# First expert layer hands twelve scatters instead of eight to the weight chain behind it; the chain's third-round loads wait for scatters, and rows are measured by halves

## The reference, cut to what matters

```
x = x + tanh(g_xattn[0]) * _L0_xattn_ref(_layernorm(x), ctx, ...)
x = x + tanh(g_ffn[0])   * _L0_ffn_ref(_layernorm(x), ...)      # 16 experts, 6 per row, and a shared expert
x = x + tanh(g_xattn[1]) * _L1_xattn_ref(_layernorm(x), ctx, ...) # 16 heads, latent keys and values
...
```

## Time and profile before

| | us |
|---|---|
| median of 3 runs | 963.36 |
| lowest, highest | 956.77, 964.65 |
| the profiled execution's own time | 961.0 |
| its span | 959.2 |

### The profile page before, as it was taken

The page is one execution under the profiler, slowest core; times in us unless marked ns, Lnnn a source line. Parts: engine busy times, 40 slices in busy tenths (PEclk is TensorE's granted clock), DMA queues, the critical chain, the costliest instruction groups (busy, mean ns, idle before and its releaser), DMA issues. The chain is left out here.

```text
span 959.2 us, 15375 instructions
## 1 busy us (share of the span) xinstructions
PE 895.2 (93%) x5046; PEld 711.2 (74%) x5046; DVE 585.4 (61%) x1069; ACT 356.2 (37%) x635; POOL 448.9 (47%) x347
## 2 busy tenths in 40 slices
PE   7999999998899999999978997999889989899997
PEld 4899997885666666666757984868647868788886
DVE  6788888557544443443366988667687746582322
ACT  3454553321033333443244534444315443322321
POOL 5787784002267887887531222271038013363233
PEclk9999999997799999999888999999999998999999
DMA  8412110009647546554622001010000027753321
GB/s 321 136 52 90 46 46 1 1 21 390 260 78 167 83 75 155 83 84 59 168 88 88 1 2 39 1 40 2 1 21 34 1 74 246 242 190 51 48 42 12
DMA packets 39893, 84.86 MB, mean 88 GB/s; under 512 B 9885, under 2 KB 27677, under 8 KB 37310
## 3 DMA queue, kind: packets, MB, share of 16 engines
q1 hardware_dynamic: 23358, 64.56, 20.1%
q0 software_dynamic: 16176, 19.31, 12.3%
q10 hardware_dynamic: 288, 0.07, 0.0%
HBM read 71.23 MB, written 20.68 MB: 96 GB/s over the span
## 5 line engine op out<-in xcount | busy, mean ns | idle before, releaser
L2708 PE MATMUL ffn_GU<-ffn_W,ffn_XTB 128*128 x252 | 90.1, 480 | 1.2 <-DVE ffn_XTB L2611 0.7
L2413 POOL DMA_INDIRECT kept_MARKED<-scratch_rows,kept_IDX x63 | 62.4, 990 | 52.4 <-DMA scratch_rows<-ffn_WEIGHT 33.5
L2595 DVE TENSOR_TENSOR ffn_GB<-ffn_GU,ffn_BIAS 128x352 f32<-128x352 f32 x63 | 33.0, 524 | 86.5 <-PE ffn_GU L2708 86.5
L1922 POOL DMA_INDIRECT out_x<-ffn_YB,ffn_XB x23 | 38.4, 1671 | 71.7 <-DVE ffn_YB L2086 53.9
L2708 PEld LDWEIGHTS ffn_GU<-ffn_W,ffn_XTB 128*128 128x128 f32 x252 | 43.2, 189 | 33.5 <-issue 19.3
L2739 PE MATMUL ffn_DN<-ffn_W,ffn_HT 96*128 x252 | 64.9, 380 | 0.0
L2451 ACT ACTIVATE ffn_HG<-ffn_GB 128x176 f32<-128x176 f32 x63 | 22.0, 350 | 96.3 <-DVE ffn_GB L2595 96.3
L358 POOL TENSOR_TENSOR attn_RP<-attn_RP,attn_RS 128x512 f32<-128x512 f32 x32 | 40.6, 1291 | 32.8 <-DVE attn_RS L525 32.8
L2064 DVE TENSOR_TENSOR ffn_HF<-ffn_GU,ffn_HG 128x512 f32<-128x512 f32 x23 | 15.9, 690 | 65.1 <-ACT ffn_HG L1943 65.0
L2739 PEld LDWEIGHTS ffn_DN<-ffn_W,ffn_HT 96*128 96x128 f32 x252 | 43.0, 190 | 3.6
L2203 PE MATMUL ffn_DN<-ffn_WDN,ffn_HT 128*128 x184 | 43.6, 380 | 0.8 <-ACT ffn_HT L1951 0.8
(11 more groups left out here) (562 smaller groups left out, 2659.5 us busy)
## 6 DMA issues: line engine op xcount, KB each, us to landing
ffn_W<-in_f_w SPq DMA_DIRECT2D x16, 608.0 KB, 18.1
ffn_WU<-in_f_w SPq DMA_DIRECT2D x8, 1024.0 KB, 6.7
attn_W<-in_L_pairs SPq DMA_DIRECT2D x7, 1088.0 KB, 5.0
ffn_WDN<-in_f_w SPq DMA_DIRECT2D x8, 512.0 KB, 8.6
scratch_rows<-in_rows_empty SPq DMA_DIRECT2D x1, 2967.0 KB, 13.6
ffn_XB<-scratch_rows SPq DMA_DIRECT2D x23, 129.0 KB, 2.1
ffn_BIAS<-in_f_bias SPq DMA_DIRECT2D x1, 2816.0 KB, 15.5
kept_STAGE<-in_f_w SPq DMA_DIRECT2D x1, 2048.0 KB, 7.8
```

What stands on the lines that cost most here:

```text
L1922: pool.indirect_dma_start(out[:, :], bass.IndirectOffsetOnAxis(ap=XB[:, i % NB, D:D + 1].bitcast(I32), axis=0), YB[:, i % 3, :], None, bou ...
L2413: pool.indirect_dma_start(XB[:, i % NB, :], None, DR["rows0"][:, :], bass.IndirectOffsetOnAxis(ap=IDX[:, i:i + 1], axis=0)).then_inc(rows_ ...
L2595: dve.tensor_tensor(GB[:, n % 2, :], GU[:, n % 2, 0:2 * HID], BIAS[:, bass.ds(e * (2 * HID), 2 * HID)], ALU.add).then_inc(biased, 1)
L2708: last = pe.matmul(GU[:, n % 2, 0:2 * HID], XTB[:, i % 2, k * P:(k + 1) * P], flat[:, bass.ds(e * WIDTH0 + k * 2 * HID, 2 * HID)], start=k ...
```

## The change

Only the seam is touched. The expert layer issues four scatters fewer (51), so the chain issues twelve. SP waits, ahead of the third round's loads, until scatter 55 has landed (scatter `TILES0 - 8`; it is odd, so it is the 28th on `sum_b`). DVE measures the first four tiles inside the last round, ahead of `y_lo`'s last part, and the other four behind it. `g_low` of the last round comes behind the normalising of the first half and behind that of the second. ACT takes the roots between its last copies `g_hi`. PE's dummy matmuls go from ten to six.

```diff
                     def _(sp):
+                        sp.wait_ge(sums_done[(TILES0 - 8) % 2], 16 * ((TILES0 - 8) // 2 + 1))
                         for g in range(2, ROUNDS):
...
                             for h in range(4):
                                 act.wait_ge(g_ps, 4 * g + h + 1)
                                 act.activation(g_part(g, h, 0), g_bank(h), ACT.Copy).then_inc(g_hi, 1)
-                        early_root(act, measured, rooted)
-                        act.wait_ge(measured, T)
-                        nrm["deviation"](act)
+                                if g == ROUNDS - 1 and h == 0:
+                                    early_root(act, measured, rooted)
+                                if g == ROUNDS - 1 and h == 1:
+                                    act.wait_ge(measured, T)
+                                    nrm["deviation"](act)
...
+                        def measure_half(h):
+                            dve.wait_ge(added, h + 1)
+                            for t in range(T // 2 * h, T // 2 * (h + 1)):
+                                measure(dve, stats, t).then_inc(measured, 1)
...
                             dve.tensor_copy(BT[:, :, :].rearrange("p a n -> p (a n)"), PB[:, 2, :]).then_inc(bt_sb, 1)
+                            if g == ROUNDS - 1:
+                                measure_half(0)
                             dve.wait_ge(y_hi, g + 1)
...
-                        for t in range(T):
-                            if t % (T // 2) == 0:
-                                dve.wait_ge(added, t // (T // 2) + 1)
-                            measure(dve, stats, t).then_inc(measured, 1)
-                            if t == T // 2:
-                                g_low(ROUNDS - 1, 0)
-                                g_low(ROUNDS - 1, 1)
+                        measure_half(1)
                         normalise(0)
+                        g_low(ROUNDS - 1, 0)
+                        g_low(ROUNDS - 1, 1)
                         normalise(1)
...
-                        keep_busy(pe, PB[:, 3, :], 10)
+                        keep_busy(pe, PB[:, 3, :], 6)
...
-            IN_STAGE = 55
+            IN_STAGE = 51
```

## The result

The changed kernel takes 973.74 us (median of 4 runs, 972.67 to 978.81) against 963.53 before (956.77 to 964.65); the ratio is 1.0136 with a 95% interval of 1.0106 to 1.0166, so it is slower by 1.1 to 1.7%. The profiled execution took 974.66 us, with a span (first to last instruction) of 972.9; before, these were 961.0 and 959.2.

A forecast was written before the change was run, and what follows sets the result against it. The train of scatters, not PE's chain, was taken as the bound: +7.8 us for it, 0 for tail and clock, made 961.0 into 968.8 (runs' median 963.36 into 971.2); 970.0 was predicted between them, range 961.5 to 976.0.

The forecast's parts named there:

- Four scatters leave the expert layer: At the expert layer's end: POOL can start the chain's small instructions earlier, gaining 0.3 us, bounds 0 and 0.5.
- The same four at the head of the train: At the chain's start: 51 starts at 455.0, 55 at 464.2 and 56 at 466.1, 9 us behind before.
- SP's new wait: Ahead of the third round's loads: they go out at 467.4, and PE should not stall.
- The other seven scatters: Scatters 56 to 62, beside twice the load: 62 starts at 483.3, and the train ends 7.8 us later.
- The pace under the double load: DMA queues beside the scatters: engines alternate queues by packet, so 6.1 us for two scatters would hold.
- Rival 2: In the scatter train: the loads block scatters wholly, 56 and 58 until about 481; +11 us, 973.2; chance 0.22.
- The rows by halves: DVE's tail behind the second half's arrival: same instructions in another order, 10.0 us; gain 0, bounds -0.5 and +0.5.
- PE's clock: In the attention's first matmuls: PE starts at half clock again; change 0, bounds -3 and +3 us.

The follow-up runs named there:

- e_hold4: The changed kernel, but the fourth round's weight loads wait until all scatters have landed; one execution, 984.3 us, beside a median of 970.97 for the kernel before.
- i_holdall: The changed kernel, but all of the chain's own loads wait until all twelve scatters have landed; one execution, 981.0 us, beside 970.97 for the kernel before.
- f_sums_first: The kernel before, but SP loads the sums ahead of the fourth round's weights; ratio 1.0103 against before.
- h_measure_early: As f_sums_first, with the changed kernel's tail and both halves of the rows measured inside the last round; ratio 1.0104 against before.
- a_move: The kernel before with only the number of scatters in the expert layer changed, from 55 to 51; ratio 1.0101 against before.
- warm: The kernel before with 28 dummy matmuls instead of ten ahead of PE's turning of rows and 12 more behind it; ratio 0.9983 against before.
- b_move_wait: The kernel before with 51 scatters in the expert layer and SP's new wait, keeping the old tail; ratio 1.0133 against before.
- c_tail: The kernel before with the rows by halves, roots, `g_low` order and six dummies, 55 scatters in the expert layer, no new wait; ratio 1.0042 against before.
- c_again: The same edit as c_tail, run once more; ratio 1.0026 against before.
- d_wait: The kernel before with only SP's wait for scatter 55 added; ratio 1.0017 against before.

## Why the prediction was right and wrong

The direction was right, and so was what bounds the stage: the train of scatters, not PE's chain. The time lies in the range (973.74, forecast 970.0, range to 976.0), but I put most of the chance on a difference within 1%, and it is beyond. What was missed in the profiled execution (968.8 forecast, 974.66 measured) is 3.0 us in the train, 0.4 in the landing of the sums and 2.5 outside the stage.

- *Four scatters leave the expert layer*: right. POOL stood idle and the stage began no earlier (454.82, before 453.35); 51 starts 1.67 us behind the stage's start, forecast 1.65.
- *The same four at the head of the train*: right. 55 and 56 are within 0.2 us of the forecast.
- *SP's new wait*: right. Loads out at 13.5 us behind the start (forecast 14.1), sections in time, PE without a stall.
- *The other seven scatters*: this is the step that failed. I kept the pace of 6.1 us, which the trace of before shows beside three sections, for six in one block and let the last pair run in 5.0. It measured 7.1, 9.6 and 3.7: 3.2 us more. e_hold4 fits that the fourth round's sections in the block make the difference (16.1 instead of 20.4), and i_holdall that loads are what stretches it (11.1 from 56 to 62 without them): I had allowed the loads a toll of 6.1 us (17.2 less 11.1), and it was 9.3. Against the same load-free train, three sections alone cost 4.7 to 4.9 us (f_sums_first, h_measure_early, e_hold4), three and three spaced ones 6.3 to 7.7 (7.3 before, 7.7 in a_move, 6.3 in warm) and six in one block 9.0 and 9.2 (b_move_wait, after). So the toll goes with the loads and not with the number of scatters beside them, and the block adds to it. Even the toll of before, 7.3, would have left 2.0 of the 20.4 us unforecast. Why a block costs more than spaced loads is not shown.
- *The pace under the double load*: by the Trainium skill (DMA: Bandwidth & Descriptors, Queues, rings and completion order) an engine takes turns between queues by packets. What I drew from it, that the pace would stay at 6.1, did not hold (7.1 and 9.6); no run shows how the packets took turns. Rival 2, by which 56 and 58 land only when the block is over, was nearer in time (973.2, and 11 us for the train where 10.8 were measured) and wrong in detail: 58 could start at 474.5, with two sections of the third round and all of the fourth still to land, so 56 had not waited for them; only 58 was held to the block's end, and 60 started at 484.1, when all had landed.
- *The rows by halves*: 0 us in the stage, as forecast, by c_tail, c_again and b_move_wait. What c_tail's ratio of 1.0042 comes from is open.
- *PE's clock*: it was at 1.2 GHz in the attention's first matmuls before and after, so the change is 0, as forecast.
- *Outside the stage*: 2.5 of the 13.7 us of the profiled pair lie there, where d_wait and c_tail also differ from before by up to 3.7 us on code that is the same. I counted on none.

## What to carry to other kernels

Before work is moved across a seam, ask which of the streams that meet behind it ends last: here PE had 7 us to spare and the scatters none, so moving work to them from where they cost nothing cost 2.4 to 2.8 us each. Small DMAs that wait for each other paid here for each group of large loads, spaced or not, and most for one block; hold a load back only if the place to which it moves has nothing that waits for small ones. And a transfer that is put ahead of another on one queue delays it by its own wait and by its bytes (9.3 and 5.2 us for the fourth round's first section in f_sums_first), so a new order of loads needs the landing time of the last one, not of the first.

## What was not expected of the hardware

An empty scatter, which moves almost nothing, took POOL the same 1.54 us for its descriptors as a full one, and beside a block of six sections the next one on its sum could start only 9.6 us later, against 3.7 with no load. A 672 KB load landed in 5.3 us with nothing ahead of it and in 10.3 and 10.5 us with 2 MB ahead, of weights or of sums. And the profiled executions of programs that differ in a few instructions of one stage differed by 3.7 us ahead of that stage and by 3.3 behind it (c_tail against before), over all runs, chips and batches even by 6.2 (453.35 us before, 459.58 in warm) and 7.1 (455.2 us in a_move, 462.3 in c_again). That is as much as most of the effects looked for here.
